# Attention with chosen key chunks and a mixture of experts on one core: the inverse root by one guess and a quartic in two factors, and the choice of chunks with the own chunk in the sort

## The chip, the cores and the metric

The kernel runs on one NeuronCore of a Trainium2 chip. The metric is the device time of one execution in microseconds (us), lower is better. The five engines that the text names are PE (TensorE, matmuls), DVE (VectorE), ACT (ScalarE), POOL (GpSimd) and SP (SyncE, which here only issues DMAs).

## The reference, cut to what matters

```python
x = hidden_states                                  # (8, 512, 256), 8 sequences
# attention: 32 heads of 8, chunks of 32 keys, 4 chunks chosen for each query and head
q, k, v = heads(x @ Wq.T), heads(x @ Wk.T), heads(x @ Wv.T);  q, k = rope(q), rope(k)
gate = einsum('bshd,bnhd->bhsn', q, kmean)         # kmean: mean of k over each of 16 chunks
gate = where(future, -1e30, gate); gate = where(own_chunk, +1e30, gate)
allowed = one_hot(top_k(gate, 4)).any() & causal
p = softmax(where(allowed, q @ k.T / sqrt(8), -1e30));  o = p @ v
rms = rsqrt(mean(o * o, axis=-1) + 1e-6)           # over the 8 of a head
o = o * rms * o_norm_weight * sigmoid(x @ Wg1.T @ Wg2.T)
x = layernorm(x + o @ Wo.T)                        # (x - mean) / sqrt(var + 1e-5)
# feed-forward: 2 shared experts and 4 of 16 routed ones, width 176
x = layernorm(x + x + shared(x) + sum_of_gated_experts(x))
```

## The kernel before, in words

The eight sequences are taken one after the other, in "turns" of about 180 us. A turn b computes the attention of sequence b, and between its matmuls the feed-forward of sequence m = b - 1, in 25 chunks of 128 hidden columns. Turn 0 has attention alone, and behind turn 7 stands a tail with the feed-forward of sequence 7. Every engine has its own program, written out by hand (`turn` in each block), and works through it in order; nothing sets the order but that text and the semaphores. `link(ins)` puts a drain of DVE behind an instruction, where the next one needs its result.

A turn has these stages. *Head:* `rope`, the transposes of q, the chunk means, the layernorm of the attention's output (`layernorm(x1n, x1n, dve_ln)` at the end of DVE's turn), its transposes and the router. *Choice:* for the query tiles j = 1, 2, 3 DVE adds a mask to the gates (`best`), takes the eight greatest of each head (`MAX8`) and marks the chosen chunks in `cbias` (`select`, in two parts, with the gating of feed-forward chunks, `gated`, between them). Meanwhile PE transposes q and k for the heads (`stack`) and computes the chunks (`up`, `down`); a chunk goes PE `up`, ACT `relu`, DVE `gated`, ACT `high`, POOL `low`, PE `down`. *Maxima:* 40 units of scores (`max_unit`), of which DVE takes the greatest of each chunk of keys (L1340). *Bias:* DVE turns the maxima into a bias, and `finish(m)` does the second layernorm of sequence m. *Attention:* eight groups of four heads. For each, PE computes five units of scores (`key_unit`, L504), ACT takes their exponents (L989), POOL masks the diagonal (`affine_select`, L1088), PE multiplies by v (`outputs`, L713), DVE copies the bank out of PSUM (`copy_outputs`, L1360), PE transposes that copy (`to_tokens`, L723) and DVE keeps it (`keep`, L1365).

There is one bank, `BK_PV`, for the products with v. So `outputs` of the next group waits for `copy_outputs` of this one (`dve_o`), and in PE's order `to_tokens`, which waits for the same copy, stands ahead of it.

`two_groups(i)` runs four times in a turn. It keeps group 2i, copies group 2i+1 (the odd copy), keeps it, squares and sums, copies group 2i+2 (the even copy), and then does the rest of the root mean square for both groups: 128 partitions x 32 numbers. The root is a guess from the bits (`root_guess`, two instructions), a quadratic step (`refine`, four) and one Newton step (`newton`, three), each linked to the one ahead. The denominator of the softmax is the ninth column of `vst`, a column of ones, and its square times 8e-6 stands for the reference's 1e-6. `layernorm` uses the same three functions on 128 x 4 numbers. POOL copies v into `vst` as a product with that column (`stage`, L1080).

The choice before: the own chunk is masked out of the gates (-1e30), `want` is the third greatest of the rest, `under` marks gates less than it, `eq` those equal to it. A running count of `eq` within each head, compared with `need`, tells which of the equal ones are left out. The marks are multiplied by `sm_h`, which is 0 at the own chunk and -OFF elsewhere.

## Time and profile before

| | us |
|---|---|
| median of 3 runs | 1547.78 |
| lowest and highest of them | 1541.15 and 1549.93 |
| the profiled execution | 1541.77 |
| its span, first to last instruction | 1539.7 |

Busy shares of the span: PE 89%, DVE 76%, ACT 55%, POOL 36%. PE's busy time is modelled and counts overlapping matmuls in full, so 89% is not a rate. The profile is read from the waits: a table of who waited for whom, the instructions in order of time (which give for each its start, its duration, and in brackets how long its engine had been idle and what ended that), and the chain that ended last. In that chain PE has 41% of the span and DVE 36%. Durations of small DVE instructions follow one another with a gap of 0.07 to 0.08 us where a drain stands between them.

### The profile page before, as it was taken

The numbers are of one execution on the slowest core, as the hardware profiler recorded it, in microseconds if no ns is written. First come the engines' busy times: TensorE is split into PE (matmuls) and PEld (weight loads), VectorE is DVE, ScalarE is ACT, GpSimd is POOL, SyncE is SP. The second block draws the span as 40 slices with busy tenths as digits, with TensorE's granted clock in tenths as the row PEclk, the third lists the DMA queues.
The fourth block names the chain that finished last, engine by engine and source line by source line (L and its number), as shares of the span: only waits on it lengthen the run. The fifth ranks groups of instructions, "written<-read, shape, count | busy, mean of one in ns | idle before, by whom it ended". The sixth has DMA issues, their size and how long they took to land.

```text
span 1539.7 us, 29870 instructions
## 1 busy us (share of the span) xinstructions
PE 1373.1 (89%) x11220; PEld 756.7 (49%) x11220; DVE 1170.6 (76%) x2931; ACT 845.4 (55%) x1266; POOL 550.0 (36%) x638
## 2 busy tenths in 40 slices
PE   5587999999998899989999899989999899998697
PEld 3322565526653366534654266543664346552364
DVE  7993789867897688967898678976889668885534
ACT  5407663395625766286643956357662776438221
POOL 4204442254323442254322543235422443225143
PEclk8757999999999999999999999999999999999798
DMA  6001022200221021210122002210112102220031
GB/s 242 8 7 16 29 71 66 45 29 20 83 66 43 15 57 63 67 24 29 63 70 50 17 28 83 65 46 17 50 62 69 30 15 59 72 52 15 14 105 61
DMA packets 52212, 77.85 MB, mean 51 GB/s; under 512 B 6322, under 2 KB 26724, under 8 KB 51812
## 3 DMA queue, kind: packets, MB, share of 16 engines
q1 hardware_dynamic: 52068, 75.94, 16.8%
q8 instruction: 89, 1.46, 0.4%
q14 instruction: 55, 0.45, 0.1%
HBM read 67.00 MB, written 8.65 MB: 49 GB/s over the span
## 4 chain that ended last, share of the span: by engine, by line
PE 41%; DVE 36%; issue 8%; DVEq 5%; ACT 4%; POOL 4%; DMA 2%; SPq 0%; POOLq 0%
PE PS L570 10%; PE PS L558 7%; DVE CM L1340 6%; PE PS L713 5%; PE PS L487 4%; POOL hp L1045 4%; DVE hr L1141 3%; DVE ropeb L1360 3%; DVEq L1133 3%; PE PS L775 2%; DVE CM L1261 2%; ACT hp L849 2%; PE PS L401 2%; PE PS L723 2%; PE PS L504 2%
## 5 line engine op out<-in xcount | busy, mean ns | idle before, releaser
L1045 POOL TENSOR_TENSOR hp<-hr,hp 128x512 f16<-128x512 f32 (+1 forms) x200 | 237.2, 1186 | 601.7 <-ACT hp L849 569.7
L1340 DVE TENSOR_REDUCE CM<-PS 128x32 f32<-128x1024 f32 x320 | 378.2, 1220 | 29.0 <-PE PS L487 25.5
L570 PE MATMUL PS<-W,hp 128*128 128x256 f16 (+1 forms) x2400 | 314.1, 274 | 22.9 <-POOL hp L1045 20.6
L558 PE MATMUL PS<-x1T,W 128*128 128x512 f16 (+1 forms) x1200 | 307.9, 383 | 0.0
L570 PEld LDWEIGHTS PS<-W,hp 128*128 128x128 f16 (+1 forms) x2400 | 214.6, 98 | 109.9 <-POOL hp L1045 49.7
L849 ACT ACTIVATE hp<-hr 128x512 f16<-128x512 f32 (+1 forms) x178 | 112.6, 633 | 240.2 <-DVE hr L1141 225.3
L840 ACT ACTIVATE hr<-PS,CF 128x512 f32<-128x512 f32 (+1 forms) x200 | 136.8, 684 | 178.7 <-PE PS L558 173.4
L1141 DVE TENSOR_TENSOR hr<-hr,gB 128x512 f32<-128x512 f32 x176 | 128.9, 732 | 72.3 <-ACT hr L840 67.6
L989 ACT ACTIVATE UK<-PS 128x1024 f32<-128x1024 f32 x160 | 153.3, 1037 | 20.8 <-PE PS L504 19.4
L558 PEld LDWEIGHTS PS<-x1T,W 128*128 128x128 f16 (+1 forms) x1200 | 107.5, 99 | 109.3 <-issue 30.0
L989 ACT ACTIVATE UQ<-PS 128x1024 f32<-128x1024 f32 x160 | 154.1, 1036 | 12.4 <-PE PS L504 10.1
L1088 POOL TENSOR_SCALAR_AFFINE_SELECT UK<-UK 128x512 f32<-128x512 f32 x128 | 85.5, 691 | 159.4 <-ACT UK L989 159.4
L504 PE MATMUL PS<-qET,kz 64*128 64x512 f16 (+3 forms) x1024 | 112.6, 307 | 25.0 <-ACT UK L989 12.0
L487 PE MATMUL PS<-kz,qET 64*128 64x512 f16 (+3 forms) x1024 | 133.5, 321 | 0.0
L504 PEld LDWEIGHTS PS<-qET,kz 64*128 64x128 f16 x1024 | 32.0, 94 | 166.6 <-ACT UK L989 62.6
L1088 POOL TENSOR_SCALAR_AFFINE_SELECT UQ<-UQ 128x512 f32<-128x512 f32 x128 | 79.8, 646 | 65.4 <-ACT UQ L989 65.4
L1360 DVE COPY ropeb<-PS 128x512 f32<-128x512 f32 x64 | 44.0, 688 | 77.5 <-PE PS L713 76.9
L713 PE MATMUL PS<-UK,vst 128*9 128x512 f32 (+3 forms) x1024 | 89.8, 446 | 0.0
L898 ACT ACTIVATE UK<-PS,CF 128x128 f32<-128x128 f32 x112 | 56.9, 527 | 54.1 <-PE PS L401 54.1
L713 PE MATMUL PS<-UQ,vst 128*9 128x512 f32 (+3 forms) x1024 | 84.8, 437 | 0.0
L1061 POOL TENSOR_TENSOR UQ<-UK,UQ 128x512 f16<-128x512 f32 x32 | 40.5, 1265 | 108.8 <-ACT UQ L885 108.8
L933 ACT ACTIVATE kz<-PS 128x1024 f16<-128x1024 f16 x64 | 65.2, 1019 | 13.1 <-PE PS L457 13.1
(157 smaller groups left out, 1963.5 us busy)
## 6 DMA issues: line engine op xcount, KB each, us to landing
gB<-gates SPq DMA_DIRECT2D x64, 256.0 KB, 3.3
gB<-gates SPq DMA_DIRECT2D x32, 224.0 KB, 2.9
gB<-gates SPq DMA_DIRECT2D x32, 192.0 KB, 2.8
gB<-gates SPq DMA_DIRECT2D x32, 160.0 KB, 2.6
xT<-in_xT SPq DMA_DIRECT2D x8, 512.0 KB, 4.0
qET<-rows SPq DMA_DIRECT2D x16, 256.0 KB, 5.2
v<-in_x SPq DMA_DIRECT2D x8, 512.0 KB, 4.0
gB<-gates SPq DMA_DIRECT2D x32, 128.0 KB, 2.9
```

Source lines behind the costliest of these rows:

```text
L487: mm = pe.matmul(PS[:, r + half, o:o + w], qET[rows, a, t * P:(t + 1) * P], kz[rows, a, 0:w], start=False, stop=True, skip_group_check=Tru ...
L504: mm = pe.matmul(PS[:, r + half, o:o + w], kz[rows, a, t * P:(t + 1) * P], qET[rows, a, t * P:S], start=True, stop=True, tile_position=(64 ...
L558: mm = pe.matmul(PS[0:w, BK_H[c % 2], :], W1[:, a, k, bass.ds(f0, w)], x1T[:, e, k, :], start=(n == 0), stop=(n == 5))
L570: mm = pe.matmul(PS[:, BK_Y + j // 2, (j % 2) * D:(j % 2 + 1) * D], hp[0:w, slot, a, j * P:(j + 1) * P], W2[0:w, e, bass.ds(c, 1), :].rear ...
L713: mm = pe.matmul(PS[32 * hh:32 * hh + HD + 1, BK_PV, t * P:S], vst[:, gs % 2, t, hh, :], PT[gs % 2][:, hh, o:o + w], start=(n == 0), stop= ...
L840: nc.scalar.activation(hr[0:w, slot, :], PS[0:w, BK_H[c % 2], :], ACT.Relu, bias=bias).then_inc(act_h, 1)
L849: nc.scalar.activation(hp[0:w, slot, 0, :], hr[0:w, slot, :], ACT.Copy).then_inc(s_high, 1)
L989: nc.scalar.activation(dst, src, ACT.Exp, scale=SCALE).then_inc(act_p, 1)
L1045: nc.gpsimd.tensor_tensor(hp[0:w, slot, 1, :], hr[0:w, slot, :], hp[0:w, slot, 0, :], ALU.subtract).then_inc(pool_hp, 1)
L1088: nc.gpsimd.affine_select(block, block, [[0, HG], [1, P]], ALU.is_ge, zero, base=0, channel_multiplier=-1).then_inc(pool_p, 1)
L1141: nc.vector.tensor_tensor(hr[:, slot, :], hr[:, slot, :], gB[:, r, :], ALU.mult).then_inc(dve_h, 1)
L1340: nc.vector.tensor_reduce(dst, src, AX.X, ALU.max).then_inc(dve_cm, 1)
```

## The change

Four edits. (1) `root_guess`, `refine` and `newton` become one function `inverse_root`: one guess in one instruction, and a quartic written as two quadratic factors, the two of them computed one behind the other with no drain between (`w`, `z`). (2) `vst`'s ninth column holds `DENOM`, the root of 8e-6, so that the nine kept numbers of a head are squared and summed in one pass; the square of the denominator and the instruction that added it are gone. The even copy moves from ahead of the root into it, behind `z`. (3) The own chunk gets +1e30 in the mask `gm_c` and takes part in the sort; `want` is the fourth greatest; `need` is subtracted from the first `eq` of each head ahead of the running count, so that a count above zero marks what is left out; the marks are 1 and 0, and the factor -OFF moves to where they are used: ACT's copy `stage_sel` and DVE's bias. `sm_c` and `sm_h` are gone from the constants. (4) POOL copies v with a `tensor_scalar`.

```diff
-            nc.gpsimd.memset(vst[:, :, :, :, HD:HD + 1], 1.0).then_inc(s_init, 1)
+            nc.gpsimd.memset(vst[:, :, :, :, HD:HD + 1], DENOM).then_inc(s_init, 1)
-                    nc.gpsimd.tensor_tensor(vst[:, gs % 2, :, :, 0:HD], vg, ones, ALU.mult).then_inc(pool_v, 1)
+                    nc.gpsimd.tensor_scalar(vst[:, gs % 2, :, :, 0:HD], vg, 1.0, 0.0, ALU.mult, ALU.add).then_inc(pool_v, 1)
-            def root_guess(n):
...
-            def refine(n):
...
-            def newton(n):
...
+            def inverse_root(n, between=None):
+                a, y, t, w, z = (buf[:, 0:n] for buf in (ms, ry, rt, rw, rz))
+                link(nc.vector.tensor_scalar(y.bitcast(I32), a.bitcast(I32), -0.5, float(ROOT), ALU.mult, ALU.add))
                 link(nc.vector.tensor_tensor(t, y, y, ALU.mult))
                 link(nc.vector.tensor_tensor(t, t, a, ALU.mult))
+                nc.vector.scalar_tensor_tensor(out=w, in0=t, scalar=QUAD[0][0], in1=t, op0=ALU.add, op1=ALU.mult)
+                link(nc.vector.scalar_tensor_tensor(out=z, in0=t, scalar=QUAD[1][0], in1=t, op0=ALU.add, op1=ALU.mult))
+                if between is not None:
+                    between()
+                link(nc.vector.scalar_tensor_tensor(out=w, in0=w, scalar=QUAD[0][1], in1=y, op0=ALU.add, op1=ALU.mult))
+                link(nc.vector.scalar_tensor_tensor(out=y, in0=z, scalar=QUAD[1][1], in1=w, op0=ALU.add, op1=ALU.mult))
@@ layernorm @@
-                root_guess(NT)
-                refine(NT)
-                newton(NT)
+                inverse_root(NT)
@@ select @@
+                link(nc.vector.tensor_tensor(heads(eq)[:, :, 0], heads(eq)[:, :, 0], need[:, 0, :], ALU.subtract))
                 link(nc.vector.tensor_tensor_scan(count, inner[j], eq, 0.0, ALU.mult, ALU.add))
-                link(nc.vector.tensor_tensor(count, count, eq, ALU.mult))
-                link(nc.vector.tensor_tensor(heads(eq), heads(count), wide(need[:, 0, :]), ALU.is_gt))
-                link(nc.vector.tensor_tensor(under, under, eq, ALU.add))
-                ins = link(nc.vector.tensor_tensor(cbias[:, j, :, 0:w], heads(under),
-                                                   sm_h[:, j:j + 1, 0:w].to_broadcast([P, H, w]), ALU.mult))
+                link(nc.vector.scalar_tensor_tensor(out=eq, in0=count, scalar=0.0, in1=eq, op0=ALU.is_gt, op1=ALU.mult))
+                ins = link(nc.vector.tensor_tensor(cbias[:, j, :, 0:w], heads(under), heads(eq), ALU.add))
@@ two_groups @@
-                    nc.vector.tensor_tensor(sq, u8, u8, ALU.mult)
-                    link(nc.vector.tensor_tensor(tok(rt), s1, s1, ALU.mult))
+                    link(nc.vector.tensor_tensor(sq, otok, otok, ALU.mult))
                     link(nc.vector.tensor_reduce(tok(ms), sq, AX.X, ALU.add))
-                    if not last:
-                        copy_outputs(i * 2 + 2)
-                    link(nc.vector.scalar_tensor_tensor(out=tok(ms), in0=tok(rt), scalar=HD * 1e-6, in1=tok(ms),
-                                                        op0=ALU.mult, op1=ALU.add))
-                    root_guess(NT * 2 * HG)
-                    refine(NT * 2 * HG)
-                    newton(NT * 2 * HG)
+                    inverse_root(NT * 2 * HG, None if last else lambda: copy_outputs(i * 2 + 2))
```

DVE's program has 185 rows less of 1829: four in each of 32 `two_groups`, two in each of 16 layernorms, one in each of 24 choices and one at the start. The other engines' programs have as many rows as before.

On DVE, in `two_groups`, from one keep (L1365) to the two instructions with which the norm is applied; CM holds the kept numbers, rep the root's. Before:

```order
L1365 COPY CM<-PS 128x4x36
L1380 TENSOR_TENSOR CM<-CM 128x256
L1381 TENSOR_TENSOR rep<-CM 128x32
L1382 TENSOR_REDUCE rep<-CM 128x32
L1360 COPY ropeb<-PS 128x512
L1385 SCALAR_TENSOR_TENSOR rep<-rep 128x32
L1150 TENSOR_SCALAR rep<-rep 128x32
L1151 TENSOR_SCALAR rep<-rep 128x32
L1157 TENSOR_TENSOR rep<-rep 128x32
L1158 TENSOR_TENSOR rep<-rep 128x32
L1159 SCALAR_TENSOR_TENSOR rep<-rep 128x32
L1160 SCALAR_TENSOR_TENSOR rep<-rep 128x32
```

Three more of L1166 to L1168 follow there, and then L1390 and L1394. Of the change, in full:

```order
L1366 TENSOR_TENSOR CM<-CM 128x288
L1367 TENSOR_REDUCE rep<-CM 128x32
L1150 TENSOR_SCALAR rep<-rep 128x32
L1151 TENSOR_TENSOR rep<-rep 128x32
L1152 TENSOR_TENSOR rep<-rep 128x32
L1153 SCALAR_TENSOR_TENSOR rep<-rep 128x32
L1154 SCALAR_TENSOR_TENSOR rep<-rep 128x32
L1347 COPY ropeb<-PS 128x512
L1157 SCALAR_TENSOR_TENSOR rep<-rep 128x32
L1158 SCALAR_TENSOR_TENSOR rep<-rep 128x32
L1369 SCALAR_TENSOR_TENSOR CM<-CM,rep 128x32x8
L1374 SCALAR_TENSOR_TENSOR qT<-qT,CM 128x4x64
```

The even copy (COPY ropeb<-PS) has seven instructions ahead of it in place of three, and four behind it in place of twelve.

On DVE, the second part of `select` for j = 1, from the comparison that writes `under` to the marks. Before:

```order
L1279 TENSOR_TENSOR flag<-gmask,want 128x256
L1281 SCALAR_TENSOR_TENSOR flag<-CH,flag 128x256
L1282 TENSOR_TENSOR flag<-flag 128x256
L1283 TENSOR_TENSOR flag<-flag,need 128x256
L1284 TENSOR_TENSOR flag<-flag 128x256
L1285 TENSOR_TENSOR cbias<-flag,CH 128x32x8
```

Of the change:

```order
L1268 TENSOR_TENSOR flag<-gmask,want 128x256
L1270 TENSOR_TENSOR flag<-flag,need 128x32
L1271 SCALAR_TENSOR_TENSOR flag<-CH,flag 128x256
L1272 SCALAR_TENSOR_TENSOR flag<-flag 128x256
L1273 TENSOR_TENSOR cbias<-flag 128x32x8
```

Four instructions behind the running count (the second row before, the third now) have become two, and a small one has come ahead of it.

## Rows read from the trace of the kernel before

**Rows 1.** Who waited for whom, PE: total us, times, longest us.

```profile
PE PS L723 <- DVE ropeb L1360: 33.2, 32, 2.1
PE PS L570 <- POOL hp L1045: 20.6, 36, 1.1
PE PS L430 <- DVE UK L1239: 10.0, 8, 7.0
```

**Rows 2.** DVE in order of time, turn 3: start, us, [idle before]; the copies alone.

```profile
681.33 0.69 DVE L1360 COPY ropeb<-PS 128x512 f32<-128x512 f32 x1 [2.81 <-PE PS L713]
...
685.96 0.69 DVE L1360 COPY ropeb<-PS 128x512 f32<-128x512 f32 x1 [1.74 <-PE PS L713]
...
691.59 0.68 DVE L1360 COPY ropeb<-PS 128x512 f32<-128x512 f32 x1
...
696.21 0.69 DVE L1360 COPY ropeb<-PS 128x512 f32<-128x512 f32 x1 [1.58 <-PE PS L713]
```

**Rows 3.** DVE in order of time, turn 3, the root's instructions between the copies.

```profile
683.17 0.42 DVE L1380 TENSOR_TENSOR CM<-CM 128x256 f32<-128x256 f32 x1
...
683.80 0.42 DVE L1382 TENSOR_REDUCE rep<-CM 128x32 f32<-128x256 f32 x1
...
688.05 0.19 DVE L1158 TENSOR_TENSOR rep<-rep 128x32 f32<-128x32 f32 x1
688.32 0.62 DVE L1159 SCALAR_TENSOR_TENSOR rep<-rep 128x32 f32<-128x32 f32 x1
...
690.58 0.70 DVE L1394 SCALAR_TENSOR_TENSOR qT<-qT,CM 128x256 f32<-128x256 f32 x1
...
693.02 0.31 DVE L1365 COPY CM<-PS 128x144 f32<-128x144 f32 x1 [0.75 <-PE PS L723]
```

**Rows 4.** POOL in order of time, turn 3, two of its diagonal masks.

```profile
688.26 0.64 POOL L1088 TENSOR_SCALAR_AFFINE_SELECT UK<-UK 128x512 f32<-128x512 f32 x1 [0.59 <-ACT UK L989]
...
695.42 1.81 POOL L1088 TENSOR_SCALAR_AFFINE_SELECT UQ<-UQ 128x512 f32<-128x512 f32 x3 [1.69 <-ACT UQ L989]
```

**Rows 5.** ACT in order of time, turn 3: the exponents of one group.

```profile
696.51 4.69 ACT L989 ACTIVATE UK<-PS 128x1024 f32<-128x1024 f32 x5
```

**Rows 6.** PE in order of time, transposes of the first copy, turns 1 and 7.

```profile
315.66 0.66 PE L723 MATMUL PS<-CF,ropeb 128*128 128x128 f32 x4 [0.34 <-DVE ropeb L1360]
...
1398.39 1.11 PE L723 MATMUL PS<-CF,ropeb 128*128 128x128 f32 x4 [1.50 <-DVE ropeb L1360]
```

**Rows 7.** DVE in order of time, the last layernorm, two of its root's instructions.

```profile
1533.27 0.16 DVE L1157 TENSOR_TENSOR rep<-rep 128x4 f32<-128x4 f32 x1
1533.51 0.16 DVE L1158 TENSOR_TENSOR rep<-rep 128x4 f32<-128x4 f32 x1
```

**Rows 8.** PE in order of time, turn 4's head and choice.

```profile
731.49 0.66 PE L430 MATMUL PS<-CF,UK 128*128 128x128 f32 x4 [0.43 <-DVE UK L1239]
...
753.90 1.48 PE L570 MATMUL PS<-W,hp 128*128 128x256 f16 x12 [0.86 <-POOL hp L1045]
```

**Rows 9.** DVE in order of time, turn 0's choice, j = 1 and j = 3.

```profile
48.33 0.29 DVE L1282 TENSOR_TENSOR flag<-flag 128x256 f16<-128x256 f16 x1
48.69 0.42 DVE L1283 TENSOR_TENSOR flag<-flag,need 128x256 f16<-128x256 f16 x1
...
64.64 0.43 DVE L1282 TENSOR_TENSOR flag<-flag 128x512 f16<-128x512 f16 x1
65.14 0.69 DVE L1283 TENSOR_TENSOR flag<-flag,need 128x512 f16<-128x512 f16 x1
```

**Rows 10.** DVE in order of time, small ones of turn 3's choice, without a drain between.

```profile
563.58 0.19 DVE L1273 TENSOR_SCALAR want<-CM 128x32 f32<-128x32 f32 x1
563.68 0.21 DVE L1274 TENSOR_TENSOR need<-CM 128x32 f16<-128x32 f32 x1
```

**Rows 11.** PE and DVE in order of time, turn 4: the first maxima.

```profile
777.11 0.39 PE L487 MATMUL PS<-kz,qET 64*128 64x512 f16 x2
...
778.11 4.68 DVE L1340 TENSOR_REDUCE CM<-PS 128x32 f32<-128x1024 f32 x4
```

More of the change, by code:

```diff
@@ L1452 @@
     n = np.arange(NCH)[None, None, :]
-    cf[:, C_GM:C_GM + 64] = np.where(n < own, 0.0, -BIG).reshape(P, -1)
-    cf[:, C_SM:C_SM + 64] = np.where(n == own, 0.0, -OFF).reshape(P, -1)
+    cf[:, C_GM:C_GM + 64] = np.where(n < own, 0.0, np.where(n == own, BIG, -BIG)).reshape(P, -1)
     ch = np.zeros((P, H_W), np.float16)
@@ L1458 @@
     ch[:, H_RST:] = np.concatenate([np.tile(np.arange(w) != 0, H) for w in (2 * CPT, 3 * CPT, 4 * CPT)])
-    ch[:, H_SM:H_SM + 64] = np.where(n == own, 0.0, -OFF).reshape(P, -1)
     cg = np.zeros((P, G_W), f32)
```

50 lines of the change are left out of this document (19 added, 31 removed).

## Prediction

> **What bounds the kernel now.** I read first who waited for whom, then the instructions of one turn in order of time. No engine is the bound throughout: PE is near its own pace in most stages, and it stands still where a DVE chain is late. Three of its waits lead to lines that the change touches [rows 1]: the transposes behind the copies of the products with v (L723, 33.2 us in 32 waits), the down products (L570, 20.6 in 36, of which one in each of turns 1 to 7 follows the choice), and the transposes of q behind the first layernorm (L430, 10.0 in 8; 7.0 of it is turn 0's start, which stays, so 3.0 in seven).
>
> The attention stage is where most is at stake. The copies of turn 3 [rows 2] come at 681.33, 685.96, 691.59, 696.21: steps of 4.63, 5.63, 4.62. Where DVE is free, and has waited for PE (1.74, 1.58 in brackets), a group takes 4.63. Where the copy has no bracket DVE itself was late, and the step is 1.0 longer. Behind the even copy (685.96) stand twelve instructions of root and norm, and the odd copy (691.59) behind them. That holds back PE, which has the transposes and the next products behind that copy, and through PE's scores ACT too.
>
> **The change part by part.**
>
> *Root in the attention.* Linked instructions on 32 numbers follow each other every 0.27, as those at 688.05 and 688.32 [rows 3]. Two unlinked ones start 0.10 apart [rows 10]. Behind the even copy stood ten small instructions (2.7) and two wide ones (1.0: as wide as the square, so 0.42 each, and 0.08 of gap), 3.7 without holds. The trace has 4.9 from the copy's end to the odd copy (685.96 + 0.69 to 691.59); the other 1.2 is holds and the keep. Now two small and two wide ones stand there, 1.5, and with the same 1.2 it is 2.7. The copy's step is 4.63, less 0.69 for the copy, so DVE is ready 1.2 early. The odd copy then goes when PE is done with the products.
>
> What is late next is the even copy, which now has the guess, two products, `w` and `z` ahead. From the keep at 693.02 the square starts after 0.40 (0.31 and the gap); square and reduction take 0.42 each [rows 3] with 0.08 behind, and 0.03 more each for 288 numbers in place of 256: 1.06. Then 0.27 for the guess and each product, 0.10 to `z`, 0.27 for `z`: 1.18. The copy could go at 693.42 + 2.24 = 695.66. It went at 696.21, when PE was done [rows 2]. Slack 0.55.
>
> Against that slack stand holds by POOL. L1159, 0.19 without disturbance as L1158, took 0.62 at 688.32 while POOL masked from 688.26 to 688.90, and ended 0.04 behind it [rows 3, 4]; L1394, as wide as the square's 0.42, shows 0.70. A hold costs 0.43. POOL's three masks start at 695.42, 0.79 ahead of the even copy: `w` and `z` (695.29 and 695.39 by the sum) fall on their start. None held leaves the copy in time; two held make it 0.3 late (0.86 less 0.55). I take 0.2 on each of 24 even copies, 4.8 in all, and for the range 0 and 0.7 (three held: 1.29 less 0.55).
>
> Sum: 33.2 less the seven first copies of turns 1 to 7 (0.34 in turn 1, 1.50 in turn 7 [rows 6], 8.6 together) is 24.6 in 25 waits. Of this, 1.6 stays in the last turn, where no projection of a next sequence stands between copy and transpose (about 0.8 for each of two, the copy's 0.69 and its signal). 24.6 - 1.6 - 4.8 = **18.2**; ends 23.0 and 6.2. ACT does not stop it short of that: it takes 4.69 for five exponents, the last one's tail under the next group's first [rows 5], and the step of 4.63 was measured with ACT in it. Nothing below 4.63 is to be gained, as there ACT and PE are both full.
>
> *Root in the layernorms.* Linked instructions on 4 numbers come every 0.24 [rows 7]. Nine become seven, one pair unlinked: 0.48 + 0.14 = 0.62. The second layernorm (`finish`) stands ahead of the first copy; each of seven waits there shrinks by up to 0.62, two of them (0.34 and 0.46) wholly: 0.8 + 5 x 0.62 = **3.9**. Above it lies 8.6, if holds that fell in the dropped instructions go too; below, 2.0. The first layernorm stands ahead of `rope` and PE's wait at L430, 0.43 [rows 8], less than 0.62, in seven turns: **3.0** (2 to 4). Spare matmuls fill the time before, so the rest of 0.62 stays hidden under them; were they not there it would be gained as well. In the tail nothing covers either layernorm: 2 x 0.62 = **1.2**. The last root of turn 7 is open too, from keep to norm: the combining product, the shift and three of Newton go, `z` comes for 0.10, the rest of 0.06 is the wider square: 5 x 0.27 - 0.10 - 0.06 = 1.2, of which I take **1.0**.
>
> *Choice.* Of the four instructions behind the running count, the multiply, the add and the marks take 0.29 and the comparison 0.42 at j = 1; 0.43 and 0.69 at j = 3 [rows 9]; 0.08 behind each. Now: a small one ahead, 0.21 as its like on 32 numbers [rows 10] and 0.07; one with a scalar, which I put at the comparison's 0.42, between that and 0.29 since no such form on two f16 inputs stands in the trace at this width; and one add. j = 1: 1.61 becomes 0.28 + 0.50 + 0.37 = 1.15, saved 0.46 (0.59). j = 3: 2.30 becomes 1.56, saved 0.74 (1.0). j = 2 between, 0.60. In turn 0 all three lie open on DVE, since PE and ACT there have only transposes and wait for the maxima: **1.8** (2.4). In turns 1 to 7 only j = 1 is on the path, through the next `gated`, ACT, POOL to PE's wait of 0.86 [rows 8]: 7 x 0.46 = **3.2**, ends 1 and 6. j = 2 and most of j = 3 lie under PE. The end of j = 3 delays the first maxima: PE was done at 777.50, DVE started at 778.11 with no idle time [rows 11]. Of 0.6 I take 0.25, as DVE and PE alternate there: **1.8** over seven turns (0 to 4.2).
>
> *At nothing.* POOL's copy of v loses one input. Behind it POOL waits for ACT, 0.59 and 1.69 in the brackets [rows 4], which hides a change of its length; were that gone, a copy longer or shorter by 0.3, half of a mask's 0.64, would be worth 64 x 0.3 = 19 either way. The scale in ACT's copy and in DVE's bias is a constant in the same instruction. The one instruction and 48 KB less at the start: under 0.3.
>
> Total 18.2 + 3.9 + 3.0 + 1.2 + 1.0 + 1.8 + 3.2 + 1.8 = **34**. The profiled execution took 1541.8, 2.1 more than its span, and would take 1508. It lies 6 under the median of the runs, 1547.8, which is what is predicted: **1513**.
>
> **The rivals.**
>
> *R1, the even copy is the new wait.* All that POOL's masks meet is held, so that three of the moved instructions are: 0.7 late, 24 x 0.7 = 17 in place of 4.8, gain 22, time 1526. For it: the masks start 0.79 ahead of that copy. Against: an instruction held behind one mask gets in ahead of the next, and the burst's first mask meets at most two of them. The Trainium skill ("SBUF — State Buffer", section "Who interferes with whom") says that a DVE instruction with two SBUF inputs, or in a two-port mode, and a GpSimd instruction that reads SBUF shut each other out for the whole instruction, whoever is first; by that rule every one of guess, products, `w` and `z` can be held, and the trace agrees with its 0.62 in place of 0.19.
>
> *R2, slower.* The same mechanism in full: each of six (square, guess, two products, `w`, `z`) held at 0.43: 2.58 less 0.55, 2.0 late, 24 x 2.0 = 49. The rest of the sum without the 4.8 is 39, so 10 slower, 1558. It decides from 1.6 late for each even copy. Against it: POOL's four masks of a group take 2.45 of 4.63 [rows 4], and the burst begins only behind the first four of the six. Little chance.
>
> *R3, nothing is given back.* No hold, all of the waits go: 23.0 + 8.6 + 4 + 1.2 + 1.2 + 2.4 + 6 + 4.2 = 51, time 1497.
>
> *R4, the choice and the layernorms bring nothing*, since PE's program behind them is as long as before and only the wait moves: 18.2 + 1.8 + 2.2 remain, 22: time 1526.
>
> **How the numbers follow.** The forecast (gain 27 to 45) 0.66; R1 or R4 (8 to 27) 0.17, R1 0.10 of it; R3 (over 45) 0.10; between -8 and 8, which needs R1 beyond its bound, 0.05; R2 0.02. A measurement of this kernel can tell about 0.5%, 8 us. Faster 0.93, same 0.05, slower 0.02. The range reaches from R3 to just beyond R1, 1495 to 1530, the three runs' own spread of 9 included.
>
> **What would show it.** The copies of a turn should come in even steps near 4.63, first odd ones (right: no wait at L723 over 0.2 but in the last turn). PE's wait behind the copies should fall from 33 to under 12. The even copy without idle time ahead would speak for R1, with 0.6 in place of 0.19 on the instructions before it. The waits at L430 should be gone, the 0.86 at the down product should be 0.4, and the second part of each choice shorter by 0.46 to 0.74. The forecast is wrong if ACT or POOL, and not DVE, turns out to have held the odd copy, or if the new two-input forms cost twice the comparison's 0.42.

## The result and the profile after

| | before | after |
|---|---|---|
| median, us | 1546.46 (4 runs) | 1498.26 (4 runs) |
| lowest and highest | 1541.15, 1549.93 | 1497.55, 1501.32 |
| the profiled execution | 1541.77 | 1497.55 |
| its span | 1539.7 | 1495.8 |

The ratio of the times is 0.9697 (95% interval 0.9674 to 0.972): 3.0% faster, 48 us between the medians and 43.9 between the two profiled spans (the profiled execution of the kernel before lies 4.7 under its median, that of the changed one 0.7). The forecast was 1513 with a range of 1495 to 1530, and a gain of 34.

PE's waits, the rows that answer to [rows 1] (total us, times, longest), with two that stand beside them:

```profile
PE PS L572 <- POOL hp L1047: 19.5, 43, 0.9
PE PS L506 <- ACT UK L991: 12.0, 25, 0.7
PE PS L534 <- DVE gsp L1198: 8.3, 8, 1.3
...
PE PS L432 <- DVE UK L1227: 7.7, 4, 7.0
...
PE PS L725 <- DVE ropeb L1347: 1.6, 2, 0.8
```

The wait behind the copies fell from 33.2 to 1.6, and what is left are the last turn's two. That of the transposes of q fell from 10.0 to 7.7, of which 7.0 is turn 0's start. The down products' total hardly moved (20.6 in 36 waits to 19.5 in 43), though the single wait behind the choice of turn 4, 0.86 in [rows 8], is 0.43 now. Seven of the waits are new, 0.24 each, ahead of the first maxima; the last part says where they come from.

DVE's copies in turn 3 of the changed kernel, in order of time (start, us, [idle before]), the rows that answer to [rows 2, 3]; POOL's masks between them are those of [rows 4]:

```profile
663.44 0.69 DVE L1347 COPY ropeb<-PS 128x512 f32<-128x512 f32 x1 [2.81 <-PE PS L715]
...
664.88 0.31 DVE L1352 COPY CM<-PS 128x144 f32<-128x144 f32 x1 [0.75 <-PE PS L725]
665.28 0.46 DVE L1366 TENSOR_TENSOR CM<-CM 128x288 f32<-128x288 f32 x1
...
667.25 0.19 DVE L1154 SCALAR_TENSOR_TENSOR rep<-rep 128x32 f32<-128x32 f32 x1
667.58 1.81 POOL L1089 TENSOR_SCALAR_AFFINE_SELECT UQ<-UQ 128x512 f32<-128x512 f32 x3 [1.19 <-ACT UQ L991]
...
668.07 0.69 DVE L1347 COPY ropeb<-PS 128x512 f32<-128x512 f32 x1 [0.63 <-PE PS L715]
...
672.90 0.69 DVE L1347 COPY ropeb<-PS 128x512 f32<-128x512 f32 x1 [2.07 <-PE PS L715]
```

The even copy (668.07) waits 0.63 for PE, the odd one (672.90) 2.07: neither is late. The steps are 4.63 and 4.83, where the odd step was 5.63. `z` ends at 667.44, 0.14 ahead of POOL's three masks, so nothing of the moved work is held.

Where the 43.9 of the spans went, from the starts of DVE's instructions that bound each stage (before less after, summed over the turns):

| stretch | gain | forecast |
|---|---|---|
| first to eighth copy | 22.6 | 18.2 |
| `finish` to first copy | 10.9 | 3.9 |
| attention's output to router | 4.3 | 3.0 |
| choice, turn 0; turns 1 to 7 | 1.5; 2.1 | 1.8; 3.2 |
| maxima, turn 0; turns 1 to 7 | 1.3; -1.1 | none; 1.8 |
| bias to first copy, turn 0 | -1.0 | none |
| eighth copy to the output, turn 7 | 1.7 | 1.0 |
| behind the last output | 1.3 | 1.2 |
| all else, 0.8 of it ahead of the first choice | 0.4 | none |

Two executions differ by some us whatever was edited. The granted clock shows much of why. Windows of the changed kernel from `finish` to the first copy, turns 4 and 5 (length, busy times, then PEclk):

```profile
826.50:835.00 8.50, 6.94 (x63) 1.54 (x62) 6.43 (x22) 7.79 (x9) 4.59 (x8) 0.80 0.03 9
1002.50:1009.80 7.30, 5.59 (x63) 1.49 (x62) 6.21 (x22) 7.28 (x9) 3.70 (x7) 1.00 0.00 1
```

In turn 4 the clock is at its lower level for a part of the stretch, and the first copy comes 1.1 later than in turn 5, of which 0.25 comes back in the next step (4.70 in place of 4.95). Such pieces fall in other groups in each execution: in two attention stages here, in three in the profile of before, in none in that of `long_root` below. In turn 7 of the kernel before one made a step of 4.63 into 6.09. In its turns 1 and 3 they fell beside the second layernorm, where DVE's chain is the path, and cost nothing: `finish` to the first copy was 0.3 and 0.2 shorter there.

Three rows of the table are the clock's in whole or in part. First turn 0, its maxima and then its bias up to the first copy. Before:

```profile
67.00:116.90 49.90, 41.85 (x218) 11.43 (x218) 46.96 (x41) 2.05 (x2) 0.00 (x0) 0.50 0.04 12
116.90:134.70 17.80, 11.41 (x78) 3.28 (x78) 3.92 (x9) 10.73 (x14) 4.08 (x8) 0.58 0.22 29
```

The changed kernel:

```profile
64.70:113.30 48.60, 39.32 (x218) 10.82 (x218) 46.67 (x41) 2.05 (x2) 0.00 (x0) 0.58 0.04 12
113.30:132.10 18.80, 12.40 (x78) 3.32 (x78) 3.92 (x9) 10.97 (x14) 4.51 (x8) 0.54 0.19 29
```

Before, the lower level (0.50) held through all of the maxima but for less of the second stretch. In all fourteen profiles of this text the maxima of turn 0 take 48.3 to 48.6 where the lower level holds for under 42 of them, and 49.6 to 49.9 where it holds for 46 or more; and the second stretch grows from 17.8, with 15.0 at the lower level, to 19.2, with 18.2. So the 1.3 and the -1.0 are not the change's. Then the output behind the eighth copy of turn 7: it takes 10.6 in this profile of before, but 9.2 in three kernels below with the same root there (`ln_only`, `choice_only`, `pool_copy`), and 8.9 here against 8.2 in `attn_only` and `copy_back`. The root's own part is 1.0, as forecast.

At these places and in the attention stages the lower clock lengthened the span of before by about 3.7 (1.3 + 1.4 + 1.5 - 0.5) and that of the changed kernel by about 3.4 (1.0 + 0.7 + 1.7 for its two pieces). This is an estimate from the differences given here; by it, the clock nearly cancels in the 43.9. Sums over turns are read with that in mind, and the medians of several rounds stand beside them.

### The profile page after: what moved, and what is told of

It is laid out like the page before. It is cut to its first block, busy times and chain, and to the rows that moved or that the text cites. A ratio compares the mean times of both kernels' runs of the same rounds, so it can differ in the third digit from the quotient of the medians.

```text
span 1495.8 us, 29484 instructions
## 1 busy us (share of the span) xinstructions
PE 1364.3 (91%) x11220; PEld 754.5 (50%) x11220; DVE 1107.3 (74%) x2746; ACT 840.4 (56%) x1266; POOL 538.3 (36%) x638
## 4 chain that ended last, share of the span: by engine, by line
PE 45%; DVE 25%; ACT 13%; issue 7%; POOL 4%; DVEq 3%; DMA 2%; SPq 1%; POOLq 0%
PE PS L572 10%; PE PS L560 8%; PE PS L715 7%; ACT UQ L991 7%; DVE CM L1327 6%; POOL hp L1047 4%; PE PS L489 4%; PE PS L506 3%; DVE hr L1140 3%; ACT UK L991 2%; ACT hp L851 2%; DVE CM L1249 2%; PE PS L777 2%; PE PS L725 2%; PE PS L397 2%
## 5 line engine op out<-in xcount | busy, mean ns | idle before, releaser
L1047 POOL TENSOR_TENSOR hp<-hr,hp 128x512 f16<-128x512 f32 (+1 forms) x200 | 241.0, 1205 | 593.3 <-ACT hp L851 561.4
L572 PE MATMUL PS<-W,hp 128*128 128x256 f16 (+1 forms) x2400 | 314.1, 274 | 21.5 <-POOL hp L1047 19.5
L991 ACT ACTIVATE UQ<-PS 128x1024 f32<-128x1024 f32 x160 | 150.9, 1041 | 3.4 <-PE PS L506 1.9
L1089 POOL TENSOR_SCALAR_AFFINE_SELECT UK<-UK 128x512 f32<-128x512 f32 x128 | 78.6, 639 | 148.7 <-ACT UK L991 148.7
```

Source lines behind the costliest of these rows:

```text
L572: mm = pe.matmul(PS[:, BK_Y + j // 2, (j % 2) * D:(j % 2 + 1) * D], hp[0:w, slot, a, j * P:(j + 1) * P], W2[0:w, e, bass.ds(c, 1), :].rear ...
L991: nc.scalar.activation(dst, src, ACT.Exp, scale=SCALE).then_inc(act_p, 1)
L1047: nc.gpsimd.tensor_tensor(hp[0:w, slot, 1, :], hr[0:w, slot, :], hp[0:w, slot, 0, :], ALU.subtract).then_inc(pool_hp, 1)
L1089: nc.gpsimd.affine_select(block, block, [[0, HG], [1, P]], ALU.is_ge, zero, base=0, channel_multiplier=-1).then_inc(pool_p, 1)
```

## The experiments

Four questions: which edit brought what, whether the even copy's move or the shorter root freed the odd copies, why the second layernorm gave three times its instructions, and what bounds the attention stage now. "The changed kernel" is at 1498.3 throughout. The kernel before was timed again in each round, with medians from 1546.5 down to 1542.9; by the ratios, the differences from the changed kernel are up to 3 larger than those of the medians.

### Each edit alone

```diff
@@ attn_only: two_groups and vst as changed; layernorm, select as before @@
+                    link(nc.vector.tensor_tensor(sq, otok, otok, ALU.mult))
+                    link(nc.vector.tensor_reduce(tok(ms), sq, AX.X, ALU.add))
+                    inverse_root(NT * 2 * HG, None if last else lambda: copy_outputs(i * 2 + 2))
```

> The kernel before with the new root in two_groups alone: nine squares, the scaled denominator (and POOL's copy of v as a tensor_scalar, since the ninth column is no longer one), the quartic, and the even copy behind z. Layernorms and choice as before. Theory S (slack: even copies lose nothing, since w and z end ahead of POOL's masks, and the odd copies lose all of their lateness): 22.5 between first and eighth copies and 1.7 behind the last, gain 24, time 1522. The count on record: 18.2 + 1.0 = 19, time 1527, with even copies 0.2 late. The rival in which three of the moved instructions are held: gain 7, time 1539.

Measured: 1518.2, ratio 0.9823 (0.9808 to 0.9838), 27 faster. Odd steps 4.83, copies 23.0 sooner in all. Theory S, and a little over. In an undisturbed turn the copies take 31.9 in place of 34.5.

```diff
@@ ln_only: layernorm alone @@
-                root_guess(NT)
-                refine(NT)
-                newton(NT)
+                inverse_root(NT)
```

> The kernel before with the new root in the two layernorms alone. The count on record: 3.9 + 3.0 + 1.2 = 8, time 1538. Theory P (phase: the four applies of the second layernorm, starting 1.0 or so earlier, end ahead of POOL's burst of three masks and run in 1.38 in place of 2.33): stretch from finish to the first copy 9.2 to 7.3 in six of seven turns, 10.9 in all, with 4.3 at the first layernorms and 1.3 in the tail: gain 16, time 1530.

Measured: 1527.9, ratio 0.9883 (0.9864 to 0.9902), 18 faster (15 to 21). `finish` to the first copy lost 8.1 in seven turns (1.34 where no low clock interferes), the first layernorms 3.1. Theory P in direction: more than twice the count on record. But here the applies take 1.70, not 1.38; they are only half out of the masks' way. Their start is 0.71 sooner than in the kernel before, where it is 0.95 sooner in the changed kernel.

```diff
@@ choice_only: select, gm_c, the marks 1 and 0 with -OFF where they are used @@
+                link(nc.vector.tensor_tensor(heads(eq)[:, :, 0], heads(eq)[:, :, 0], need[:, 0, :], ALU.subtract))
                 link(nc.vector.tensor_tensor_scan(count, inner[j], eq, 0.0, ALU.mult, ALU.add))
+                link(nc.vector.scalar_tensor_tensor(out=eq, in0=count, scalar=0.0, in1=eq, op0=ALU.is_gt, op1=ALU.mult))
+                ins = link(nc.vector.tensor_tensor(cbias[:, j, :, 0:w], heads(under), heads(eq), ALU.add))
```

> The kernel before with the new choice alone (own chunk in the sort, need subtracted ahead of the count, marks 1 and 0). The count on record: 1.8 + 3.2 + 1.8 = 6.8, time 1539.5. Theory M (the marks' last addition meets POOL's products where the multiply by the mask did not, and the first maxima are not earlier in turns 1 to 7): choice 2.1 in seven turns, turn 0 1.5, maxima nothing: gain 3 to 4, time 1543.

Measured: 1541.2, ratio 0.9977 (0.9963 to 0.9991), 3.6 faster. Theory M. The maxima of turns 1 to 7 are 0.14 longer each in this kernel too.

```diff
@@ pool_copy: POOL's stage alone @@
-                    nc.gpsimd.tensor_tensor(vst[:, gs % 2, :, :, 0:HD], vg, ones, ALU.mult).then_inc(pool_v, 1)
+                    nc.gpsimd.tensor_scalar(vst[:, gs % 2, :, :, 0:HD], vg, 1.0, 0.0, ALU.mult, ALU.add).then_inc(pool_v, 1)
```

> The kernel before with POOL's copy of v as a tensor_scalar, nothing else. The count on record: nothing, between -1 and 1, since POOL waits for ACT behind it. Rival Q: the copy is 0.13 shorter 64 times and reads one input in place of two, so that DVE instructions beside it are held less; then up to 64 x 0.13 = 8 faster.

Measured: 1537.9, ratio 0.9951 (0.9933 to 0.997), 7.6 faster (4.6 to 10.3), where the count said nothing. The odd steps are 5.37 in place of 5.63. Turn 3 of this kernel, POOL and DVE behind an even copy:

```profile
685.08 0.30 POOL L1079 TENSOR_SCALAR vst<-v 128x128 f32<-128x128 f32 x1
685.23 0.18 DVE L1150 TENSOR_SCALAR rep<-rep 128x32 int32<-128x32 int32 x1
...
686.09 0.64 POOL L1087 TENSOR_SCALAR_AFFINE_SELECT UK<-UK 128x512 f32<-128x512 f32 x1 [0.72 <-ACT UK L989]
686.29 0.48 DVE L1159 SCALAR_TENSOR_TENSOR rep<-rep 128x32 f32<-128x32 f32 x1
```

The same place in the kernel before:

```profile
687.25 0.42 POOL L1080 TENSOR_TENSOR vst<-v,vst 128x128 f32<-128x128 f32 x1
687.40 0.31 DVE L1151 TENSOR_SCALAR rep<-rep 128x32 int32<-128x32 int32 x1
```

POOL's own wait for ACT did cover the copy on POOL. But DVE's second instruction of the guess lay beside it and was held, 0.31; it now takes 0.18. Started 0.13 sooner, the next instruction that meets a mask is held for 0.48 and not 0.62 as in [rows 3]. Together that is the 0.26 of two odd steps in each turn, 4 us in all; the third, 4.76, is as before. `finish` to the first copy is 0.12 shorter.

The three whole edits give 27 + 18 + 4 = 49 against the changed kernel's 47 by its ratio, so they add up. The copy of v is part of the first.

### Even copy moved, or root shortened

```diff
@@ move_only: the kernel before, the even copy inside the old root @@
-                    if not last:
-                        copy_outputs(i * 2 + 2)
@@ refine @@
                 link(nc.vector.tensor_tensor(t, y, y, ALU.mult))
+                if between is not None:
+                    between()
                 link(nc.vector.tensor_tensor(t, t, a, ALU.mult))
```

> The kernel before with one edit: the even copy stands behind the first product of the old root (the combining product, the guess and y times y ahead of it, nine small instructions and two wide ones less these behind). Theory B (balance: the lateness was one of placing, since DVE waited 1.74 at the even copies and was 1.0 late at the odd ones): 1.06 to 1.4 of work moves ahead of the even copy, which stays in time, and the odd copies lose 0.9 to 1.0 of their lateness: 18 faster, time 1527, steps of 4.6 to 4.8. Theory L (the root had to become shorter; holds of 0.43 by POOL eat what the move gives): even copies without bracket, odd steps still over 5.2, gain 8 or less, time 1537 or more.

Measured: 1520.5, ratio 0.9856 (0.9834 to 0.9878), 22 faster. Steps 4.63 and 4.83 in every turn, as in the changed kernel. Turn 5, the copies (odd, even, odd, even):

```profile
1030.81 0.69 DVE L1362 COPY ropeb<-PS 128x512 f32<-128x512 f32 x1 [2.81 <-PE PS L713]
...
1035.44 0.69 DVE L1362 COPY ropeb<-PS 128x512 f32<-128x512 f32 x1 [0.68 <-PE PS L713]
...
1040.27 0.69 DVE L1362 COPY ropeb<-PS 128x512 f32<-128x512 f32 x1 [0.40 <-PE PS L713]
...
1044.89 0.69 DVE L1362 COPY ropeb<-PS 128x512 f32<-128x512 f32 x1 [0.68 <-PE PS L713]
```

Not one instruction of the old root is gone, and no copy is late. Theory B. The lateness of 1.0 came from where the copy stood.

```diff
@@ copy_back: the changed kernel, the even copy ahead of the root @@
-                    inverse_root(NT * 2 * HG, None if last else lambda: copy_outputs(i * 2 + 2))
+                    if not last:
+                        copy_outputs(i * 2 + 2)
+                    inverse_root(NT * 2 * HG)
```

> The changed kernel with the even copy back ahead of the root (behind the reduction), all else as changed. In the changed kernel's trace DVE has waited 2.07 at the odd copies and 0.63 at the even ones. Theory W (the shorter root alone is enough; the move adds nothing): four instructions at 0.27 and one at 0.10 move behind the copy, 1.18 of the 2.07, so the odd copies stay in time: no difference from the changed kernel, 1498, up to 1.5 either way. Theory V (the move is needed): by the count on record the odd copy would be ready 3.9 behind the even one, just as PE is, and holds of 0.43 make it late in most of 25 steps: 5 to 10 slower, 1503 to 1508, with no bracket at the odd copies.

Measured: 1500.6, ratio 0.9719 (0.9701 to 0.9737), 2.3 over the changed kernel with intervals that overlap (its profile has three pieces of the lower clock ahead of first copies, and its span is 0.9 longer). Turn 2, an even and an odd copy:

```profile
493.51 0.69 DVE L1347 COPY ropeb<-PS 128x512 f32<-128x512 f32 x1 [1.79 <-PE PS L715]
...
495.82 0.64 POOL L1089 TENSOR_SCALAR_AFFINE_SELECT UK<-UK 128x512 f32<-128x512 f32 x1 [0.71 <-ACT UK L991]
495.85 0.65 DVE L1158 SCALAR_TENSOR_TENSOR rep<-rep 128x32 f32<-128x32 f32 x1
...
498.34 0.69 DVE L1347 COPY ropeb<-PS 128x512 f32<-128x512 f32 x1 [0.44 <-PE PS L715]
```

The odd copy still has 0.44 to spare, though a mask holds one of the root's instructions (0.65). Theory W: either half of the edit is enough, and the other then brings nothing there. Only the last group of each turn is touched: its step is 3.85 in place of 3.77.

```diff
@@ long_root: all edits but the shorter root in two_groups; the even copy as in move_only @@
```

> The kernel before with every edit but the shorter root in two_groups: the even copy stands behind the first product of the old root; the new root in the layernorms, the new choice and POOL's new copy are in. Theory R (redundant: with the even copy moved, the shorter root and the nine squares bring only the last root of turn 7, 1.2 to 1.7): 1500, odd steps 4.83 as in the changed kernel. Rival (the old root leaves DVE too near the edge once the rest is faster): odd copies without bracket in several turns, 1504 or more.

Measured: 1500.6, ratio 0.972 (0.9691 to 0.9748). Odd steps 4.83, and behind the last copy of turn 7 it is 1.25 longer than the changed kernel. Theory R: of the attention's shorter root and nine squares, the last root of turn 7 is what remains.

```diff
@@ pool_back: the changed kernel, POOL's copy a product again @@
-                    nc.gpsimd.tensor_scalar(vst[:, gs % 2, :, :, 0:HD], vg, 1.0, 0.0, ALU.mult, ALU.add).then_inc(pool_v, 1)
+                    nc.gpsimd.tensor_tensor(vst[:, gs % 2, :, :, 0:HD], vg, ones1[:, :, :, :].to_broadcast([P, NT, HG, HD]),
+                                            ALU.mult).then_inc(pool_v, 1)
```

> The changed kernel with POOL's copy of v as a product again, with a column of ones of its own (0.43 in place of 0.30, two inputs). Theory C (cover: DVE now has 2.07 and 0.63 to spare at the copies, so what that copy holds is hidden there, and only the second layernorm can feel it, 0.1 to 0.3 in each of seven turns): 0.5 to 2 slower, 1499 to 1500. Theory A (the 7 that this edit alone gave in the kernel before are its own, POOL's or PE's): 5 to 8 slower, 1503 to 1506.

Measured: 1502.1, ratio 0.9724 (0.9696 to 0.9753), 3.8 over the changed kernel, intervals overlapping. In the trace the copies' steps are the same. `finish` to the first copy is 7.84 in place of 7.29: the applies start 0.24 later, 6.05 behind the start of `finish` and not 5.82, meet the masks, and take 1.70. The next step is 4.63 in place of 4.95, so 0.2 is lost in a turn, 1.6 in all. The trace speaks for theory C; the times lie between the two, and can't tell 1.6 from 6.

### The second layernorm

`finish` to first copy took 9.2 before and 7.3 after, 1.9 less for 0.62 of instructions (turn 5 below, 9.5 before, had one more hold). Turn 5 of the kernel before, the applies (four of 128x256) and POOL:

```profile
1034.45 1.91 POOL L1088 TENSOR_SCALAR_AFFINE_SELECT UQ<-UQ 128x512 f32<-128x512 f32 x3 [1.19 <-ACT UQ L989]
1034.65 2.29 DVE L1182 TENSOR_SCALAR x1n<-x1n,rep 128x256 f32<-128x256 f32 x4
```

Turn 5 of the changed kernel:

```profile
1008.36 1.38 DVE L1170 TENSOR_SCALAR x1n<-x1n,rep 128x256 f32<-128x256 f32 x4
1009.46 1.96 POOL L1089 TENSOR_SCALAR_AFFINE_SELECT UQ<-UQ 128x512 f32<-128x512 f32 x3 [1.19 <-ACT UQ L991]
```

The applies used to run beside POOL's three masks. They now begin 1.1 ahead of them and are nearly done. Before, they start 6.77 behind the start of `finish` and take 2.33 in the turns at the full clock but turn 5; now it is 5.82 and 1.38. So the 1.9 is 0.95 of applies that are no longer held and 0.95 of an earlier start: 0.71 from the shorter root (0.62 of instructions and 0.09 of holds) and 0.24 from POOL's shorter copy, by `ln_only` and `pool_back`. To price the place, the chain was lengthened in steps:

```diff
@@ dose_ln: layernorm, m times in finish(m) @@
                 inverse_root(NT)
+                for _ in range(more_links):
+                    link(nc.vector.tensor_tensor(rt[:, 0:NT], ry[:, 0:NT], ry[:, 0:NT], ALU.mult))
```

> The changed kernel with m additional linked products of 128 x 4 (0.24 each) behind the root of the second layernorm of sequence m, so none in turn 1 and six in turn 7 (seven in the tail). Read: the time from finish to the first copy, 7.29 now in turns 1, 2, 3, 5 and 6. Theory P (phase): with one more link the four applies meet POOL's three masks and grow from 1.38: about 7.8 at one link, 8.5 at two, 9.3 at four (1.0 of it from the applies, as 2.33 before). Theory L (length alone): 7.53, 7.77, 8.25 and the applies stay 1.38. Over the kernel P gives 10 to 12 slower than 1498, L 6 to 7.

Measured: 1509.3 in one run, 11 over the changed kernel. The stretch in turns 1 to 7 is 7.29, 8.38, 8.43, 9.07, 9.19, 9.66, 9.66, and the applies 1.38, 1.38, 2.05, 2.45, 2.33, 1.93, 1.93. (In the turn with one link the first copy waited 0.94 for PE, whose granted clock was 0.80 over the stretch.) Turn 5, four links:

```profile
1013.43 0.88 DVE L1170 TENSOR_TENSOR rep<-rep 128x4 f32<-128x4 f32 x4
1014.38 2.33 DVE L1172 TENSOR_SCALAR x1n<-x1n,rep 128x256 f32<-128x256 f32 x4
1014.53 2.04 POOL L1089 TENSOR_SCALAR_AFFINE_SELECT UQ<-UQ 128x512 f32<-128x512 f32 x3 [1.19 <-ACT UQ L991]
```

Four links of 0.96 in all bring back the 2.33 and the 9.2 of the kernel before. Theory P. The turn with one link can't be read, since the lower clock fell in it; but `pool_back` and `ln_only` have their applies at that very start, 6.05, and there they take 1.70 and the stretch 7.84, where theory P had 7.8. With five and six links the applies start later in the burst and are held less (1.93): what counts is when they start against POOL.

### The price of being late at an even copy

```diff
@@ dose_even: inverse_root in two_groups, b times in turn b @@
+                for _ in range(more_links):
+                    link(nc.vector.tensor_tensor(rt[:, 0:n], ry[:, 0:n], ry[:, 0:n], ALU.mult))
                 if between is not None:
                     between()
```

> The changed kernel with b additional linked products of 128 x 32 (0.27 each) ahead of each of the three even copies of turn b, none in turn 0. Read: the lateness of even copies (step less 4.63). Theory L (slack of 0.63 alone): nothing in turns 1 and 2, 0.18 in turn 3, then 0.45, 0.72, 0.99, 1.26 in turns 4 to 7; sum of three each 10.8, time 1509. Theory H (the second product and those behind meet POOL's burst, which starts 0.33 behind the start of z): 0.3 late in turn 2 already, 0.5 to 0.9 in turn 3, and 1.7 or more in turn 7; time 1515 or more.

Measured: 1529.9 in one run, 32 over the changed kernel. Theory H: even steps are 0.25 late with two products and 0.86 with three, where L had nothing and 0.18. An even step and the odd one behind it together (9.46 undisturbed) grow by 0.05 with two products, 0.65 with three, 1.2 with four, and 1.5 or 1.8 with five: nothing in the slack, then 0.6 for each product of 0.27 up to the fourth, and 0.3 to 0.6 behind it. Some 7 of the 32 are the clock's: in turns 6 and 7 five pieces of the lower level fell in the attention stage, 0.8 ahead of the first copy and 1.4 to 1.7 on each of four steps. Turn 5:

```profile
1036.53 0.19 DVE L1154 SCALAR_TENSOR_TENSOR rep<-rep 128x32 f32<-128x32 f32 x1
1036.55 1.84 POOL L1089 TENSOR_SCALAR_AFFINE_SELECT UQ<-UQ 128x512 f32<-128x512 f32 x3 [1.19 <-ACT UQ L991]
1036.79 2.17 DVE L1156 TENSOR_TENSOR rep<-rep 128x32 f32<-128x32 f32 x5
...
1039.04 0.69 DVE L1349 COPY ropeb<-PS 128x512 f32<-128x512 f32 x1
```

Five products that need 1.35 take 2.17 beside the three masks. So the hold that the rival R1 spoke of is real, but it lay farther off than the 0.14 between `z` and the masks: a first product more still started 0.07 ahead of them (317.29 against 317.36 in turn 1) and made no copy late, and R1's price of 0.7 is reached with three.

### What bounds the stage now

```diff
@@ dose_act: b additional copies of 128 x 32 ahead of the exponents of groups 3 to 8 of turn b @@
+                    for k in range(times):
+                        nc.scalar.activation(aside[:, k * 32:k * 32 + 32], CF[:, 0:32], ACT.Copy)
```

> The changed kernel with b additional ACT instructions (copies of 128 x 32 into a buffer of their own, not linked) ahead of the exponents of each of the third to eighth groups in turn b. Read: the steps between copies, 4.63 and 4.83 now, against the time of the additional instructions in each group. Theory A (ACT is now the bound of the stage, as its five exponents of 4.69 to 4.76 follow one another without a gap): the steps grow by the whole of that time from turn 1 on. Theory F (PE's and ACT's chain of waits has air in it): the first 0.2 to 0.4 of a group is taken up, and steps in turn 1 are as before.

Measured: 1508.3 in one run, 10 over. ACT in order of time in turn 3, three additional ones and then the exponents:

```profile
665.65 0.57 ACT L996 ACTIVATE aside<-CF 128x32 f32<-128x32 f32 x3
666.01 4.78 ACT L992 ACTIVATE UQ<-PS 128x1024 f32<-128x1024 f32 x5
```

Three of them push the exponents by 0.36, so 0.12 each and 0.24 in a pair of steps. The pair (9.46) is unchanged with one, and grows by 0.14, 0.40, 0.62 and 0.86 with two to five, 1.34 with seven: 0.24 for each beyond the first 0.34. Neither theory as written, F nearer: there is 0.17 of air in a group, and behind that ACT is the bound. The forecast's statement that nothing below 4.63 is to be gained fits, as no step between copies but the last of a turn went below it.

### A shorter router, meant to be faster

The first layernorm gave 0.61 a turn where PE's wait had been 0.43, as if DVE's chain up to the choice were the path. So the router was shortened there.

```diff
@@ short_route: route @@
-                link(nc.vector.memset(rtop[:, :, KR:8], PAD))
-                for j in range(NT):
-                    nc.vector.match_replace(rrep[:, j, :], rtop[:, j, :], sc[:, j, :], CHOSEN)
-                dve.drain()
-                link(nc.vector.scalar_tensor_tensor(out=gat[:, :, :], in0=rrep[:, :, 0:NE], scalar=BIG, in1=sc[:, :, 0:NE],
-                                                    op0=ALU.is_gt, op1=ALU.mult))
+                for j in range(NT):
+                    nc.vector.scalar_tensor_tensor(out=gat[:, j, :], in0=sc[:, j, 0:NE], scalar=rtop[:, j, KR - 1:KR],
+                                                   in1=sc[:, j, 0:NE], op0=ALU.is_ge, op1=ALU.mult)
+                dve.drain()
```

> The changed kernel with a shorter router on DVE: the gates above or equal to the fourth greatest are taken by four instructions of 128 x 16 with the fourth greatest as their scalar, in place of a memset, four replacements and a comparison (of gates that are exactly equal at the fourth place, it keeps all, where the reference keeps the first). In the changed kernel's trace of turn 4 the replaced part takes 2.2 (715.46 to 717.69); the new one should take 0.6. Theory D (from the attention's output to the first choice DVE's own chain is the path, as the 0.61 gained at each first layernorm says, where PE's wait had been 0.43): each of seven turns 1.3 to 1.6 shorter and 1.0 in the tail, 10 to 12 faster than the changed kernel, 1487. Theory E (PE, which waits 1.3 for the router's gates in each turn, is the path behind that wait, and its feed-forward matmuls have no air): the choice starts earlier, but the maxima do not; gain 5 or less, 1494 or more.

Measured: 1513.2, ratio 0.9813 (0.9794 to 0.9831): 15 slower than the changed kernel, on the other side of both theories. Turn 4, DVE and POOL:

```profile
722.10 3.32 DVE L1188 SCALAR_TENSOR_TENSOR er<-sc,rtop 128x16 f32<-128x16 f32 x4
722.53 0.62 POOL L1057 TENSOR_SCALAR UK<-CH 128x512 f16<-128x512 f16 x1
723.11 1.16 POOL L1063 TENSOR_TENSOR UQ<-UK,UQ 128x512 f16<-128x512 f32 x1
724.23 1.16 POOL L1063 TENSOR_TENSOR UK<-UK 128x512 f16<-128x512 f32 x1
725.34 1.16 POOL L1047 TENSOR_TENSOR hp<-hr,hp 128x512 f16<-128x512 f32 x1
```

The same place in the changed kernel, its last replacement and the comparison:

```profile
716.46 1.16 POOL L1063 TENSOR_TENSOR UQ<-UK,UQ 128x512 f16<-128x512 f32 x1
716.48 0.17 DVE L1189 MATCH_REPLACE8 rrep<-rtop,sc 128x21 f32<-128x21 f32 x1
716.72 0.97 DVE L1191 SCALAR_TENSOR_TENSOR er<-rrep,sc 128x64 f32<-128x64 f32 x1
717.58 1.15 POOL L1063 TENSOR_TENSOR UK<-UK 128x512 f16<-128x512 f32 x1
```

Four instructions of 16 numbers took 3.32: their time is that of POOL's four instructions beside them, as if each got in only between two of those. The replacements that they stand for run beside POOL unhindered (0.17, as in the tail, where POOL stands still). And the 2.2 that were to be saved had been read in the one turn whose comparison was held: it takes 0.97 there and 0.23 in the other seven. So the stretch to the first choice grew by 0.8 in six of seven turns, and PE's wait for the router (L534) from 0.97 or 1.26 to 1.75. That makes 5 to 6 of the 15. A window of the choice of turn 2 shows most of the rest:

```profile
376.00:379.00 3.00, 3.00 (x15) 1.90 (x14) 2.77 (x6) 0.59 (x1) 0.73 (x1) 0.50 0.64 198
```

PEclk is 0.50, the lower level of 1.2 GHz, where the changed kernel has 1.00 over the whole choice of each turn. It fell behind the 1.75 in four of seven choices, which are 1.2 to 2.8 longer, 7.4 in all. That the longer wait is what lets the clock fall is inferred: three turns had the same wait and kept their clock.

## Why the prediction was right and wrong

**Direction and range were right, and at the copies the mechanism too.** The odd copies lost all of their lateness, the steps are 4.63 and 4.83, and the waits at the copies and at the transposes of q went as forecast. The time was 15 below the forecast, near R3's 1497. So the rival with a tenth of the chance described the outcome better, for reasons of which it knew half.

**The copies (18.2 forecast, 22.6 measured).** The eight turns without what disturbed single groups give 8 x (34.53 - 32.26) = 18.2, the forecast's figure, and that is luck: three of its terms were off and nearly cancel. The other 4.4 lie in groups that were disturbed in this one profile of before (steps of 6.18 and 6.72 in turns 0 and 2, the latter at the full clock, 6.09 in turn 7 at the lower one). The first mis-sized term is the 0.2 on each even copy, 4.8 in all. The forecast had `w` and `z` at the start of POOL's masks; they ended 0.14 ahead of them. The slack of 0.55 was right (0.63). The second is the step that the odd copies were to fall to: two of three in a turn are 4.83 and not 4.63, 3.2 in all. The third is not in the sum: with the first copy sooner, the second step is 4.95 in place of 4.63, so 0.3 a turn is given back there. Adding the first copies' share back would have been wrong as well.

**What freed them** was not told apart in the forecast. Its own numbers held the answer: 1.74 of idle time at one copy, 1.0 of lateness at the other. `move_only` put four small instructions ahead of the copy and took none away, and that was enough.

**The second layernorm (3.9 forecast, 10.9 measured)** is the largest miss. The step that failed is "each of seven waits there shrinks by up to 0.62". PE's recorded wait was taken as the most that could be won (0.34 and 0.46 in turns 1 and 3, where the clock was at its lower level), the dropped instructions as the most in the other five, and the applies as a constant. But the applies were held by 0.95, and the 0.95 by which they now start sooner freed them. The upper end, 8.6, had holds in it, yet only those of dropped instructions. The 10.9 still hides a part, since two pieces of the lower clock fell in this stretch: in `long_root`, which has none, it is 13.1 less than before, and 10.8 with the 0.3 a turn given back at the second copy taken off, over that end.

**The first layernorm (3.0, 4.3)** failed by the same cap: a gain limited to the wait of 0.43. It was the full 0.61 in most turns. The wait on that row was not the whole of what hung on the chain: PE's wait for the router's gates farther down is as long as before (0.96 and 0.97 in turn 5), so the chain from the layernorm to the router moved as a whole. Why PE's wait at the transposes showed only 0.43 of it was not settled.

**POOL's copy (nothing; 7.6 alone, 0 to 4 in the changed kernel).** The forecast named the cover on POOL and forgot the neighbour: the copy's length mattered to the DVE instruction beside it. With 2.07 to spare at the odd copies that is hidden there, but not in the second layernorm, where it is worth 0.55 of the 1.9, less the 0.3 that the next step gives back.

**The choice and the first maxima (3.2 and 1.8; 2.1 and -1.1).** The comparison with a scalar did take what was assumed (0.43 at j = 1, 0.69 at j = 3, undisturbed), and PE's wait behind j = 1 is 0.43 or less in six of seven turns, as forecast. What failed is that nothing was to be lost behind it. Turn 4 at j = 3, DVE's comparison and addition, POOL's product `low` and PE's down product:

```profile
752.99 0.69 DVE L1272 SCALAR_TENSOR_TENSOR flag<-flag 128x512 f16<-128x512 f16 x1
753.04 1.66 POOL L1047 TENSOR_TENSOR hp<-hr,hp 128x512 f16<-128x512 f32 x1 [2.25 <-ACT hp L851]
753.76 1.22 DVE L1273 TENSOR_TENSOR cbias<-flag 128x512 f16<-128x512 f16 x1
754.76 1.48 PE L572 MATMUL PS<-W,hp 128*128 128x256 f16 x12 [0.24 <-POOL hp L1047]
```

The comparison now starts 0.05 ahead of POOL's product, which takes 1.66 in place of the 1.16 that it took there before, and the addition behind it takes 1.22 where undisturbed it takes 0.43. PE waits 0.24 for that product, in each of seven turns, in `choice_only` too: more than half of the 0.43 won at j = 1 goes again. And "of 0.6 I take 0.25" at the first maxima was nothing: DVE starts its last marks 2.0 sooner, but then waits 0.95 for PE. The maxima took 0.14 more a turn as well; why was not settled.

**The rule behind R1.** R1 cited the Trainium skill ("SBUF — State Buffer", section "Who interferes with whom") for two-input instructions and two-port modes being shut out. `short_route` and `dose_even` agree with it, 3.32 for four and 2.17 for five. The same section of the Trainium skill says that a DVE instruction with at most one SBUF input, outside those modes, does not contend; the replacement of 0.17 at 716.48 beside POOL's product agrees. That section of the Trainium skill also lists `tensor_scalar` among those that can, and the applies agree: 1.38 alone, 2.45 beside the masks.

**Not settled**, besides what is said above: why single groups of the kernel before are disturbed at the full clock, which is most of the 4.4 at its copies.

## What to carry to other kernels

Where one engine serves two waits in turn, compare the idle time at one with the lateness at the other before shortening anything: placing the served instruction in the middle of the long chain gave 22 of 27 us without removing an instruction. A chain that runs beside another engine's burst has a price that depends on its start, so read what lies 1 us ahead and behind, and count instructions that can be held, not their width: four tiny ones took 3.32 where the memset and the four replacements that they stood for took 1.2. What is held can be the other engine too, and its reader behind it. A PE wait on a row is not an upper bound for what a shorter chain ahead of it brings.

## What the runs showed of the hardware

- DVE instructions of `short_route` and `dose_even` alternate with POOL's back-to-back ones: four of 128x16 took 3.32, where POOL ran four instructions of 0.62 and 1.16. Five of 128x32 beside masks of 0.64 took 2.17 in place of 1.35. The hold goes the other way where DVE starts first: POOL's product took 1.66 in place of 1.16 behind a DVE comparison that began 0.05 ahead of it.
- Four `tensor_scalar` of 128x256 f32 with two per-partition scalars took 1.38 free and up to 2.45 beside POOL. Copies out of PSUM (0.69), the four MAX8 of the router (0.41) and the replacements (0.17) take the same time with POOL busy beside them and with POOL idle.
- POOL's copy of 128x128 f32 takes 0.30 as a `tensor_scalar` and 0.43 as a product with a broadcast.
- A piece of the lower granted clock in the attention stage costs 0.8 to 1.7 where PE is waited for (0.8 and 0.9 net in turns 7 and 4 of the changed kernel, 1.5 in turn 7 of the kernel before, 1.7 on the last step of `dose_even`'s turn 7) and nothing where DVE's chain is the path (turns 1 and 3 of the kernel before). It falls in other turns in each kernel's profile.
